# Heads stage: rows turned one chunk ahead, and the mix's two parts in one pair of banks

## The reference

```python
xf = jnp.fft.fft2(x)
qf = xf.reshape(b, HEADS, hd, h * w)                 # 8 heads of 16 channels
qn = _l2norm_lastdim(qf)
attn_f = jnp.einsum('bhcn,bhdn->bhcd', qn, qn) * temp_f[None]
attn_f = jax.lax.complex(softmax(attn_f.real), softmax(attn_f.imag))
out_cplx = jnp.einsum('bhcd,bhdn->bhcn', attn_f, qf)
out_f = jnp.abs(jnp.fft.ifft2(out_cplx)).reshape(b, c, h, w)
```

## Time and profile before

| | |
|---|---|
| median of 3 runs | 24692.61 us (24690.05 to 24702.98) |
| profiled execution | 24716.94 us, its span 24715.1 us |
| TensorE (PE) busy | 22097.5 us, 89% |
| DVE busy | 20112.6 us, 81% |
| ACT busy | 13207.1 us, 53% |
| GpSimd (POOL) busy | 12334.8 us, 50%, all of it in layer 1 |
| layer 0 | about the first 43% of the span, 8 images |

### The profile page before, as it was taken

How to read it: one execution, slowest core, us unless ns; L and a number is a source line. 1 busy time by engine, 2 the same in 40 slices (tenths; PEclk the granted TensorE clock), 3 DMA queues, 4 the chain that set the end, 5 groups by cost and what they waited for, 6 DMA issues and landing times.

```text
span 24715.1 us, 342082 instructions
## 1 busy us (share of the span) xinstructions
PE 22097.5 (89%) x113121; PEld 13072.9 (53%) x113121; DVE 20112.6 (81%) x24473; ACT 13207.1 (53%) x18815; POOL 12334.8 (50%) x4613
## 2 busy tenths in 40 slices
PE   5999989898999999898888888988888888888888
PEld 4777768686877777683333333333333333333333
DVE  4666667565666666578999999999999999999999
ACT  2323131423223231416777777777777777777776
POOL 0000000000000000007999999999999999999998
PEclk8999999999999999999999999999999999999999
DMA  3132221314031222214444444444444444444444
GB/s 105 37 91 72 82 82 48 116 29 134 11 104 49 84 80 76 74 43 168 166 175 184 166 193 169 166 190 169 165 193 164 195 166 168 188 169 169 190 168 162
DMA packets 1134985, 3189.43 MB, mean 129 GB/s; under 512 B 345641, under 2 KB 617402, under 8 KB 848954
## 3 DMA queue, kind: packets, MB, share of 16 engines
q1 hardware_dynamic: 1134394, 3181.84, 35.5%
HBM read 2885.04 MB, written 296.49 MB: 129 GB/s over the span
## 4 chain that ended last, share of the span: by engine, by line
PE 33%; DVE 9%; issue 6%; ACT 4%; DMA 2%; DVEq 0%; ACTq 0%; POOL 0%; SPq 0%; POOLq 0%
PE yp L2161 16%; PE pj L2117 8%; DVE hid L2384 4%; DVE hid L2390 3%; PE pj L2146 2%; PE pj L2176 2%; PE pj L2134 2%; PE pj L2125 2%; PE yp L2153 1%; ACT t L2243 1%; DMA img<-x 1%; DMA bc<-bc_rows 1%; DVE delta L2426 1%; ACT xn L2257 1%; ACT du L2291 1%
## 5 line engine op out<-in xcount | busy, mean ns | idle before, releaser
L2492 POOL TENSOR_TENSOR hid<-hid,bc 128x2048 f32<-128x2048 f32 x2048 | 7810.0, 3813 | 908.8 <-DVE carry L2398 904.5
L2161 PE MATMUL yp<-hid,ident 128*128 128x512 f32 x16384 | 7343.5, 597 | 428.8 <-POOL hid L2492 428.7
L2466 POOL TENSOR_SCALAR_AFFINE_SELECT ident<-ident 128x128 f32<-128x128 f32 x1 | 0.3, 292 | 11210.3 <-DVE ident L2351 11210.3
L2161 PEld LDWEIGHTS yp<-hid,ident 128*128 128x128 f32 x16384 | 3039.7, 189 | 4626.0 <-issue 3959.1
L2384 DVE TENSOR_TENSOR_SCAN hid<-da,carry,t 128x512 f32<-128x512 f32 x3968 | 4856.8, 1266 | 111.1 <-DVE carry L2398 17.2
L2390 DVE TENSOR_TENSOR_SCAN hid<-t,carry,hid 128x512 f32<-128x512 f32 x3968 | 4827.5, 1258 | 29.3 <-ACT t L2232 28.1
L2485 POOL TENSOR_TENSOR hid<-bc,du 128x1024 f32<-128x1024 f32 x2048 | 4094.8, 1999 | 199.4 <-PE yp L2161 173.3
L2232 ACT ACTIVATE t<-delta,v_a 128x512 f32<-128x512 f32 x4096 | 2659.3, 681 | 1573.8 <-DVE hid L2390 1570.7
L1291 PE MATMUL bk<-region 128*128 128x256 f16 (+2 forms) x30640 | 3377.2, 266 | 36.8 <-ACT region L1657 19.2
L2117 PE MATMUL pj<-xn,w_x 128*128 128x512 f32 x4096 | 2377.3, 734 | 1079.4 <-ACT xn L2257 1031.0
L1291 PE MATMUL bk<-work,region 128*128 128x256 f16 x27336 | 3159.7, 273 | 97.8 <-DVE work L996 74.2
(11 more groups left out here) (299 smaller groups left out, 22370.8 us busy)
## 6 DMA issues: line engine op xcount, KB each, us to landing
bc<-bc_rows SPq DMA_DIRECT2D x1024, 2048.0 KB, 7.2
work<-in_shift_d SPq DMA_DIRECT2D x256, 512.0 KB, 4.5
work<-in_x SPq DMA_DIRECT2D x256, 256.0 KB, 3.0
work<-in_x SPq DMA_DIRECT2D x128, 512.0 KB, 5.3
xpad<-in_x SPq DMA_DIRECT2D x32, 2048.0 KB, 12.5
gated<-work SPq DMA_DIRECT2D x256, 256.0 KB, 2.4
region<-gated SPq DMA_DIRECT2D x256, 256.0 KB, 2.7
region<-heads SPq DMA_DIRECT2D x1024, 64.0 KB, 2.3
```

Source lines behind the costliest of these rows:

```text
L2161: m = nc.tensor.matmul(yp[:, h, :], ident[:, :], hid[:, k % 4, n, :], start=False, stop=(g == G - 1 and n == 3), skip_group_check=True)
L2492: nc.gpsimd.tensor_tensor(hid[:, k % 4, :, :], hid[:, k % 4, :, :], bc[:, g, 1, :, :], ALU.mult).then_inc(s_hc.sem, 1)
```

## The change

Three things, none of which adds or removes an instruction:

1. `turned` becomes two buffers. TensorE turns the rows of chunk n+1 before the shift product of n, and DVE copies them at the head of its work for chunk n, when the shift of n-1 is done. ACT takes the rows of n+2 at the head of its work for chunk n, ahead of the copy of the shifted real part.
2. The shift product of an even chunk writes banks 1 and 2, that of an odd chunk banks 5 and 6, and it waits for banks emptied two chunks back.
3. Both parts of the mix write banks 3 and 4. Each waits for the squares of the part directly before it (`4 * m + 2 * o`).

```diff
-        turned = wk(512, 512)
+        turned = [wk(512, 512), wk(9472, 512)]
@@ DVE
-                def turned_rows(kk):
-                    dve.wait_ge(s_tr.sem, s_tr.at(b, kk + 1))
-                    dve.wait_ge(s_sh.sem, s_sh.at(b, kk))
-                    V.tensor_copy(turned, bk[0][:, :]).then_inc(s_trc.sem, 1)
+                def turned_rows(n_, to):
+                    dve.wait_ge(s_tr.sem, s_tr.at(b, n_ + 1))
+                    dve.wait_ge(s_sh.sem, s_sh.at(b, n_ - 1))
+                    V.tensor_copy(to, bk[0][:, :]).then_inc(s_trc.sem, 1)
...
+                        re, im = bk[1 + 4 * blk][:, :], bk[2 + 4 * blk][:, :]
+                        if not (isinstance(n_, int) and n_ == NK - 1):
+                            turned_rows(n_ + 1, turned[1 - blk])
                         dve.wait_ge(s_sh.sem, s_sh.at(b, n_ + 1))
...
-                        V.scalar_tensor_tensor(to[:, 1, 1], bk[2][:, :], HSCALE, to[:, 1, 0], ALU.mult, ALU.subtract).then_inc(s_shi.sem, 1)
-                        if not (isinstance(n_, int) and n_ == NK - 1):
-                            turned_rows(n_ + 1)
+                        V.scalar_tensor_tensor(to[:, 1, 1], im, HSCALE, to[:, 1, 0], ALU.mult, ALU.subtract).then_inc(s_shi.sem, 1)
@@ TensorE
-                    pe.wait_ge(s_os.sem, s_os.at(b, 4 * m - 2 + 2 * o))
+                    pe.wait_ge(s_os.sem, s_os.at(b, 4 * m + 2 * o))
...
-                                    x_ = mm(bk[3 + 2 * o + r][64 * blk:64 * blk + 64, :], ...
+                                    x_ = mm(bk[3 + r][64 * blk:64 * blk + 64, :], ...
...
+                        if not (isinstance(n_, int) and n_ == NK - 1):
+                            turn(n_ + 1)
                         pe.wait_ge(s_trc.sem, s_trc.at(b, n_ + 1))
                         pe.wait_ge(s_kl[blk], b * (8 * NK) + m * 16 + 16)
-                        pe.wait_ge(s_shr.sem, s_shr.at(b, n_))
-                        pe.wait_ge(s_shi.sem, s_shi.at(b, n_))
+                        pe.wait_ge(s_shr.sem, s_shr.at(b, n_ - 1))
+                        pe.wait_ge(s_shi.sem, s_shi.at(b, n_ - 1))
...
-                                x_ = mm(bk[1 + s][:, j * P:(j + 1) * P], turned[:, j * P:(j + 1) * P], ...
+                                x_ = mm(bk[1 + 4 * blk + s][:, j * P:(j + 1) * P], turned[blk][:, j * P:(j + 1) * P], ...
                         x_.then_inc(s_sh.sem, 1)
-                        if not (isinstance(n_, int) and n_ == NK - 1):
-                            turn(n_ + 1)
@@ ACT
-                        cp(sq2[2 * o + r], bk[3 + 2 * o + r][:, :], ACT.Square, ...
+                        cp(sq2[2 * o + r], bk[3 + r][:, :], ACT.Square, ...
...
+                        if not (isinstance(m, int) and m == NM - 1):
+                            take_rows(n_ + 2, place(m + 1, blk))
                         act.wait_ge(s_sh.sem, s_sh.at(b, n_ + 1))
                         act.wait_ge(s_o.sem, s_o.at(b, 2 * m - 2))
-                        cp(shifted[2 * mp + blk][:, 0, 0], bk[1][:, :], scale=HSCALE).then_inc(s_shr.sem, 1)
-                        if not (isinstance(m, int) and m == NM - 1):
-                            take_rows(n_ + 2, place(m + 1, blk))
+                        cp(shifted[2 * mp + blk][:, 0, 0], bk[1 + 4 * blk][:, :], scale=HSCALE).then_inc(s_shr.sem, 1)
```

More of the change, by code:

```diff
@@ L948, in body @@
                         dve.wait_ge(s_o.sem, s_o.at(b, 2 * m - 2))
-                        V.tensor_scalar(to[:, 1, 0], bk[2][:, :], HSCALE, None, ALU.mult).then_inc(s_imh.sem, 1)
+                        V.tensor_scalar(to[:, 1, 0], im, HSCALE, None, ALU.mult).then_inc(s_imh.sem, 1)
                         dve.wait_ge(s_shr.sem, s_shr.at(b, n_ + 1))
-                        V.scalar_tensor_tensor(to[:, 0, 1], bk[1][:, :], HSCALE, to[:, 0, 0], ALU.mult, ALU.subtract)
+                        V.scalar_tensor_tensor(to[:, 0, 1], re, HSCALE, to[:, 0, 0], ALU.mult, ALU.subtract)
                         dve.wait_ge(s_imh.sem, s_imh.at(b, n_ + 1))
-                        V.scalar_tensor_tensor(to[:, 1, 1], bk[2][:, :], HSCALE, to[:, 1, 0], ALU.mult, ALU.subtract).then_inc(s_shi.sem, 1)
-                        if not (isinstance(n_, int) and n_ == NK - 1):
-                            turned_rows(n_ + 1)
+                        V.scalar_tensor_tensor(to[:, 1, 1], im, HSCALE, to[:, 1, 0], ALU.mult, ALU.subtract).then_inc(s_shi.sem, 1)
                         if blk == 0 and not (isinstance(m, int) and m < 2):
@@ L959, in body @@
                             next_rows(b + 1, n_, blk)
-                turned_rows(0)
+                turned_rows(0, turned[0])
                 heads_loop(dve, body)
@@ L1471, in mix @@
                                 for blk in range(2):
-                                    x_ = mm(bk[3 + 2 * o + r][64 * blk:64 * blk + 64, :], mix16[rows_, w_, wh, rows_], shifted[2 * mp + blk][rows_, part, ph, :], start=(n_ == 0 and wh == 0 and ph == 0), stop=(n_ == 1 and wh == 1))
+                                    x_ = mm(bk[3 + r][64 * blk:64 * blk + 64, :], mix16[rows_, w_, wh, rows_], shifted[2 * mp + blk][rows_, part, ph, :], start=(n_ == 0 and wh == 0 and ph == 0), stop=(n_ == 1 and wh == 1))
                     x_.then_inc(s_o.sem, 1)
@@ L1478, in body @@
                         n_ = 2 * m + blk
+                        if not (isinstance(n_, int) and n_ == NK - 1):
+                            turn(n_ + 1)
                         pe.wait_ge(s_trc.sem, s_trc.at(b, n_ + 1))
                         pe.wait_ge(s_kl[blk], b * (8 * NK) + m * 16 + 16)
-                        pe.wait_ge(s_shr.sem, s_shr.at(b, n_))
-                        pe.wait_ge(s_shi.sem, s_shi.at(b, n_))
+                        pe.wait_ge(s_shr.sem, s_shr.at(b, n_ - 1))
+                        pe.wait_ge(s_shi.sem, s_shi.at(b, n_ - 1))
                         for j in range(4):
                             for s in range(2):
-                                x_ = mm(bk[1 + s][:, j * P:(j + 1) * P], turned[:, j * P:(j + 1) * P], kbuf3[blk][:, j, s * P:(s + 1) * P], start=True, stop=True)
+                                x_ = mm(bk[1 + 4 * blk + s][:, j * P:(j + 1) * P], turned[blk][:, j * P:(j + 1) * P], kbuf3[blk][:, j, s * P:(s + 1) * P], start=True, stop=True)
                         x_.then_inc(s_sh.sem, 1)
-                        if not (isinstance(n_, int) and n_ == NK - 1):
-                            turn(n_ + 1)
                         if not (isinstance(m, int) and m == 0):
@@ L1748, in squares @@
                     for r in range(2):
-                        cp(sq2[2 * o + r], bk[3 + 2 * o + r][:, :], ACT.Square, scale=1.0 / (HSCALE * HWEIGHT)).then_inc(s_os.sem, 1)
+                        cp(sq2[2 * o + r], bk[3 + r][:, :], ACT.Square, scale=1.0 / (HSCALE * HWEIGHT)).then_inc(s_os.sem, 1)
                 def root(m, r, q, i_):
```

## The result

The changed kernel takes 24491.49 us (median of 4 runs, 24484.65 to 24495.51), the kernel before 24692.94 us in the same comparison: a ratio of 0.9916, interval 0.9903 to 0.9928, or 201 us less. The forecast was 24537 us, 156 us less.

The account below looks back on a forecast made before the run. No engine is full; a chain of waits on DVE's row copy and addition of squares bounds the stage. Pairs 15.6, start +4.6, stalls -0.5, end -0.2 make 19.5 us an image, x 8 = 156: 24537 us, range 24465 to 24635.

Parts of the forecast that it names:

- Step 1: Turned rows one chunk ahead, two shift bank pairs: shifts stop waiting for DVE's copies; TensorE needs 7.76 us a pair.
- step 2: Both mix parts in banks 3 and 4: part 1 waits for part 0's squares, making the pair 9.1 us, not 7.76.
- the loop: Even shift, ACT copy, DVE copies, addition, root, squares, mix part 1, turn, next shift: 9.1 us a pair instead of 10.33.
- One slack: ACT's spare time before the next even chunk's high real part: free at about 10.4, wanted at 11.3, 0.9 us spare.
- The rule on rotating banks: Independent matmul groups should rotate through PSUM banks; with the mix still rotated, the pair would be 7.76 us.
- Rival A: The mix's wait for squares does not bind; TensorE sets the pair at 7.76 us: 24410 us, chance 0.08.
- Rival B: Shifts still follow DVE's and ACT's in-order queues; the pair becomes 10.0 us: 24660 us, chance 0.11.
- rival C: Shift tables' landings stretch and set the pair; at 8.6 us landing it is 0.5 us longer: 24745 us, chance 0.07.
- The pairs as a whole: Thirteen pairs of chunks in the heads stage, each 1.2 us shorter: 15.6 us gained an image.
- first stores: Three times an image a quarter's first store delays the shift table behind it: 0.5 us lost an image, bounds 0 and 3.
- The start: Heads stage up to its fifth shift: turns and shifts run ahead, gaining 4.6 us an image, range 2 to 5.5.
- The end of the stage: From shift 30 to the next stage's first product: 0.2 us lost, bounds 0.8 gained and 1.5 lost.

Follow-up runs that it names:

- squares ahead of the root: Changed kernel with ACT's two squares of mix part 0 placed before the root in the even chunk; 24541.1 us, 0.9932 of the kernel before.
- half root: Changed kernel with each ACT root over half the elements, so half of the heads' values are not computed; 24463.6 us, 0.9900 of the kernel before.
- additions first: Changed kernel with DVE's addition of squares moved right behind the row copy in the even chunk; 24403.4 us, 0.9877 of the kernel before.
- additions first and late stores: Changed kernel with DVE's addition of squares moved right behind the row copy and SP's stores of finished heads begun two chunks later; 24388.7 us.
- rows ahead only: Changed kernel with its bank changes undone, rows still turned and copied one chunk ahead; 24585.5 us, 0.9951 of the kernel before.

## Why the prediction held, point by point

**Step 1 and step 2, the loop.** Right in its links, and 0.2 us too long. By the pair above: shift to high part 2.10 (2.17 forecast), to 953 0.64 (0.64), to the addition 1.20 (1.20), to the root 0.82 (0.82), to the squares 1.02 (1.04), to part 1 of the mix 1.20 (1.09 + 0.1), to the turn 1.42 (1.49), to the next shift 0.50 (0.53). The links add up to 8.90 us where the forecast's add up to 9.08. 0.10 us of the difference are TensorE's two terms: 1.49 is the mix's duration to its modelled end, but the turn starts 0.07 ahead of it; the shift's way to the high part is another 0.07. One slack was sized wrong: ACT has 0.45 us to spare ahead of the even chunk's copy (its row above) where 0.9 was forecast, and the run with squares ahead of the root used it up. The half root shows that the loop is the cause and not only a sum that fits. The rule on rotating banks, which the prediction weighed (the Trainium skill, "Perfetto Trace Analysis", Matmuls), is borne out as far as the wait goes, 1.24 us a pair, but that wait is the loop's and not the shared banks' alone: with additions first the mix has the same two banks, and TensorE no longer waits for ACT. Rival A, TensorE as the bound, is refuted for the changed kernel and true of the kernel with additions first. Rival B, no effect, and rival C, landings, did not come: in the changed kernel nothing in the loop waits for a table except behind a first store. At the shorter pairs of the two kernels with additions first single landings did stretch, to 5.6 us and more, and TensorE waited for them.

**The pairs as a whole** were forecast at 15.6 less 0.5 for first stores, 15.1 us an image; they gave 17.3. Most of it is the loop's length: a pair gained 1.33 us on average where 1.2 was forecast, 1.7 us in 13 pairs. The rest is that the first stores cost 0.15 us in the seventh image and less in most others, and not 0.5. The lateness of the tables was forecast well (1.1 us; TensorE waited 1.23, 0.86 and 0.58), and so was what hides it, TensorE's wait of 1.24 us ahead of the mix. How much comes through the cover varies: in the second trace of the changed kernel, of the run of 24501.5 us, TensorE waited 0.85 to 1.51 us for these tables in the first seven images, and shift 4 to 30 took 114.86 to 115.58 us against 114.69 at best, so 0.2 to 0.9 us were lost in an image. The 0.15 us were therefore partly a lucky trace, and 0.5 is not refuted as a size. Once that cover is gone, as with additions first, a late table costs its full wait, up to 1.4 us.

**The start** was the term most off: 4.6 us forecast, 7.8 measured (22.9 on average before, 15.15 after). Timeline of the changed kernel, its first shifts:

```profile
8545.69 3.78 PE L1291 MATMUL bk<-work 128*128 128x128 f32 x16 [1.84 <-DMA work<-in_shift_d]
...
8549.50 0.33 SPq L1214 DMA_DIRECT2D work<-in_shift_d  x1
...
8550.11 2.09 PE L1291 MATMUL bk<-work 128*128 128x128 f32 x16
...
8552.84 0.63 PE L1457 MATMUL bk<-ctab,work 128*128 128x128 f32 x4 [0.64 <-DVE work L931]
...
8553.31 3.37 PE L1291 MATMUL bk<-work 128*128 128x128 f32 x40
...
8560.89 3.37 PE L1291 MATMUL bk<-work 128*128 128x128 f32 x40
```

Three things. The table of chunk 2, issued at 8549.50, landed 3.1 us later, where I took the loop's median of 4.7, and shift 2 waited for a row copy instead; the trace of before already had this table landing in 3.6 us. Shift 1 ran at full clock (2.09 us), and no later product was slow, where before shift 2 took 3.11. And the seventh image, by which I counted, had a start 0.9 us shorter than the mean of before. From shift 2 on TensorE goes every 3.79 us, since there are no roots yet and so no loop.

**The end of the stage** was forecast 0.2 us longer. From shift 30 to the next stage's product it takes 24.94 us in the seventh image against 25.06: within the bounds, no change. Its two terms were both somewhat larger and cancel: shift 31 comes 1.3 us earlier behind shift 30 (3.30 us against 4.63; 0.8 forecast), and what follows it takes 1.2 us longer (1.0 forecast).

**The sum**: 7.8 + 17.3 = 25.1 an image against 19.5, x 8 = 201 against 156. The time lies within the range (24465 to 24635) and the mechanism is the forecast one; of the 45 us missing in the sum, about 26 are the start, 17 the pairs and 2 the end.

## What to carry to other kernels

When a copy is taken off the path, add up every closed loop through the engines' orders, from start to start, before believing in the busiest engine as the next bound; here the loop's sum was 9.1 us, measured 8.9, where TensorE alone needed 7.6. Ask of each link whether it has to hang where it does: the addition of squares needed nothing of the chunk behind whose copies it stood, and moving it gave another 100 us on top of the change's 200. Between shift 4 and shift 30, sharing a pair of banks cost nothing once its squares came early, and a late transfer was nearly free while it lay in front of another wait; both hold only as long as that cover does.

## What was not expected

The kernel with additions first and late stores takes 0.9870 (0.9853 to 0.9886) of the kernel before, against 0.9916 for the change. With eight banks (`bk` in the kernel), mix and shift can't be given two pairs each, as the turn needs one bank; another division was not tried. Of the chip, two things were new to me. TensorE's clock did not fall again in the start of the changed kernel: over the start it was granted 0.84 to 0.87 in the eight images, with one shift product of 3.8 us in each, where before it was 0.61 to 0.83, with two or three slow ones. With rows ahead only, where the shifts still wait for copies, there is also just one slow product; what keeps the clock up is left open. And the landing of a 512 KB table is not one number: 3.1 us for chunk 2 of the changed kernel, a median of 4.7 in the loop of before and in that of the changed kernel, 3.9 to 4.9 for the tables behind a first store, and up to 7.5 in single cases at a pair of 7.6 us. What a first store delays is the issue of the table, not its transfer.
